# Group-norm statistics sent over ScalarE's queue, with the order of VectorE, ScalarE and TensorE changed around them

## What is computed

```python
xn = group_norm(x)                      # 32 groups of 12 channels
w  = xn^T qkv_w^T                       # (n, 384), in 12 heads of 32 channels
s  = sum_d (w / norm_n(w))^2            # per point and head
Pi = softmax over the heads (s * temp)
Pn = Pi / (sum_n Pi + 1e-8)
attn = 1 / (1 + sum_n Pn * w^2)         # per head and channel
y  = x + (-(w * Pi) * attn) out_w^T + out_b
```

## Time and profile before

| | us |
|---|---|
| median of 3 runs | 910.02 (908.9 to 911.25) |
| the profiled execution | 909.34 |
| its span, first to last instruction | 907.6 |

### The profile page before, as it was taken

One profiled execution on the slowest core, in us unless ns is written; L12 is line 12 of the kernel. 1 busy time (PEld: TensorE's weight loads), 2 busy tenths in 40 slices (PEclk: granted clock), 3 DMA queues, 4 the chain that ended last, 5 costly groups with the idle time before them and its releaser, 6 DMA issues.

```text
span 907.6 us, 14234 instructions
## 1 busy us (share of the span) xinstructions
PE 861.0 (95%) x4322; PEld 687.0 (76%) x4322; DVE 743.8 (82%) x1368; ACT 523.4 (58%) x676; POOL 225.6 (25%) x101
## 2 busy tenths in 40 slices
PE   7799999999999999999999999999999999999996
PEld 6577787777777777778777778777778777778785
DVE  7588888888888888888888888888888888888755
ACT  4566555667555667555667655567655567655621
POOL 1331133332123332123332123333123333113300
PEclk9899999999999999999999999999999999999998
DMA  7314664544665544565544565544565444464432
GB/s 286 123 46 177 216 217 154 183 143 172 214 216 165 176 144 169 211 216 175 184 142 167 197 216 188 175 148 163 192 216 203 161 160 165 179 215 148 145 120 93
DMA packets 54852, 158.47 MB, mean 175 GB/s; under 512 B 21426, under 2 KB 25778, under 8 KB 50866
## 3 DMA queue, kind: packets, MB, share of 16 engines
q1 hardware_dynamic: 54688, 158.25, 51.5%
q10 hardware_dynamic: 146, 0.00, 0.0%
HBM read 105.70 MB, written 52.53 MB: 174 GB/s over the span
## 4 chain that ended last, share of the span: by engine, by line
PE 50%; DMA 16%; issue 13%; DVE 11%; ACT 7%; SPq 2%; ACTq 1%; DVEq 0%
PE acc L482 46%; DMA PIB<-pi 12%; DMA pi<-PIT 4%; PE scores L562 3%; DVE WV L778 3%; ACT WS L386 2%; ACT XH L414 2%; ACT WV L395 1%; DVE UL L788 1%; SPq L301 1%; SPq L296 1%; ACT UH L376 1%; PE acc L465 1%; DVE WS L752 1%; DVE PIT L740 1%
## 5 line engine op out<-in xcount | busy, mean ns | idle before, releaser
L336 POOL TENSOR_TENSOR XL<-XN,XH 128x1024 fp32r<-128x1024 f32 x93 | 222.6, 2408 | 617.2 <-ACT XH L414 616.2
L386 ACT ACTIVATE WS<-acc 128x1024 f32<-128x1024 f32 x96 | 97.6, 1017 | 236.2 <-PE acc L482 177.5
L482 PE MATMUL acc<-UH,W2H 128*128 128x512 f32 x576 | 179.1, 392 | 4.5 <-ACT UH L376 4.5
L482 PE MATMUL acc<-XH,W1H 128*128 128x512 f32 x576 | 178.7, 392 | 3.7 <-ACT XH L414 3.7
L482 PE MATMUL acc<-UH,W2L 128*128 128x512 f32 x576 | 178.4, 391 | 0.0
L482 PE MATMUL acc<-XH,W1L 128*128 128x512 f32 x576 | 178.2, 391 | 0.0
L796 DVE SCALAR_TENSOR_TENSOR X<-acc,bias,X 128x1024 f32<-128x1024 f32 x96 | 120.1, 1276 | 56.9 <-PE acc L482 56.8
L376 ACT ACTIVATE UH<-WV 128x1024 fp32r<-128x1024 f32 x96 | 98.1, 1054 | 108.6 <-DVE WV L778 108.3
L482 PE MATMUL acc<-UL,W2H 128*128 128x512 f32 x576 | 150.2, 396 | 0.0
L482 PE MATMUL acc<-XL,W1H 128*128 128x512 f32 x576 | 147.0, 391 | 0.0
L752 DVE CUSTOM_DVE_ANT_0 WS<-PIB,WS 128x1024 f32<-128x1024 f32 x96 | 117.2, 1223 | 23.3 <-DMA PIB<-pi 21.7
(11 more groups left out here) (78 smaller groups left out, 443.2 us busy)
## 6 DMA issues: line engine op xcount, KB each, us to landing
PIB<-pi SPq DMA_DIRECT2D x96, 528.0 KB, 6.0
out_y<-X SPq DMA_DIRECT2D x96, 512.0 KB, 6.8
X<-in_x SPq DMA_DIRECT2D x31, 1536.0 KB, 6.2
gathered<-stats_rows SPq DMA_DIRECT2D x31, 72.0 KB, 2.8
pi<-PIT SPq DMA_DIRECT2D x96, 16.5 KB
X<-in_x SPq DMA_DIRECT2D x3, 512.0 KB, 4.5
WV<-in_L_conv_qkv_w SPq DMA_DIRECT2D x1, 576.0 KB, 6.4
WS<-in_L_conv_out_w SPq DMA_DIRECT2D x1, 576.0 KB, 7.4
```

The costliest lines, as they stand in the source:

```text
L336: pool.tensor_tensor(XL[:, t, :], XN[:, t, :], XH[:, t, :].bitcast(F32), ALU.subtract).then_inc(xl_done, 1)
L386: act.activation(square_tile(i, t), acc[:, t, :], ACT.Square, accum_out=sumsq[:, t:t + 1]).then_inc(squared, 1)
L482: last = pe.matmul(out[:, h * BANK:(h + 1) * BANK], w[:, k, m * P:(m + 1) * P], r[:, k, h * BANK:(h + 1) * BANK], start=(n == 0 and k == 0 ...
```

## The change

- `write_stats` and `gather_stats` leave SP's queue for ACT's: ACT issues both at the end of its step, after XH of tile 2. The pair of image 1 stays on SP.
- ACT: `group_seeds` moves to right behind u_hi(0); in step 0 to right behind square(2).
- DVE: `group_norm` moves ahead of the u_lo's, `head_sum_weights` ahead of u_lo(2). In the step behind the last image finish(30, 2) moves behind the three weigh's.
- Image 1: XN and XL are made by DVE, in step 0 behind the softmax and ahead of the statistics of tiles 1 and 2, instead of by ACT and POOL.
- Start: the statistics of image 1 are taken before the low parts of the second weights.
- PE, in step 0: 4 idle turns ahead of the head sums and 6 behind them.

```diff
-IDLE_TURNS = (6, 3, 4, 24)
+IDLE_TURNS = (6, 3, 4, 24, 4, 6)
@@ sync, step
                 spread_pi(i)
-                write_stats(i + 2)
                 store(i - 1, 0)
                 store(i - 1, 1)
-                gather_stats(i + 2)
@@ gpsimd, x_lo and scalar, normalise
-                if has(j) and j.follows(1):
+                if has(j) and j.follows(2):
@@ scalar, step
                 u_hi(0)
+                if i.follows(1):
+                    group_seeds(i + 1)
                 square_w(1)
                 u_hi(1)
                 u_hi(2)
                 square_w(2)
+                if has(i) and not i.follows(1):
+                    group_seeds(i + 1)
                 keep_w(1)
-                if has(i):
-                    group_seeds(i + 1)
                 keep_w(2)
...
                 x_hi(2)
+                if i.follows(0):
+                    write_stats(act, i + 2)
+                    gather_stats(act, i + 2)
@@ tensor, step
                 first_product(i, 2)
+                if not i.follows(1):
+                    idle_turns(small[:, P:2 * P], IDLE_TURNS[4])
                 second_product(i - 1, 0, {(2, 0): lambda: head_sums(i)})
+                if not i.follows(1):
+                    idle_turns(small[:, P:2 * P], IDLE_TURNS[5])
@@ vector, step
                     dot(i - 1, t)
-                if not has(i) and has(i - 1):
-                    finish(i - 2, 2)
                 for k in range(4):
                     attention(i - 1, k)
                 group_moments(i + 1)
                 weigh(i - 1, 0)
                 weigh(i - 1, 1)
                 weigh(i - 1, 2)
+                if not has(i) and has(i - 1):
+                    finish(i - 2, 2)
+                group_norm(i + 1)
                 u_lo(i - 1, 0)
                 u_lo(i - 1, 1)
+                head_sum_weights(i)
                 u_lo(i - 1, 2)
-                head_sum_weights(i)
-                group_norm(i + 1)
                 group_stats(i + 2, [0])
                 softmax_shift(i)
                 softmax_divide(i)
+                if not i.follows(1):
+                    normalise(FIRST + 1)
+                    lower_x(FIRST + 1)
                 group_stats(i + 2, range(1, T))
@@ vector, start
-            normalise_first()
-            lower_first()
+            normalise(FIRST)
+            lower_x(FIRST)
+            group_stats(FIRST + 1, range(T))
             weights_lower(range(T, 2 * T))
...
-            group_stats(FIRST + 1, range(T))
             pipeline(dve, step, 0, B + 1)
```

More of the change, by code:

```diff
@@ L234, in x_tile, with write_stats, gather_stats @@
             return X[:, j.slot, t * N:(t + 1) * N]
+        def write_stats(eng, j):
+            if has(j):
+                eng.wait_ge(gn_step, j.counts(GN_STEPS, GN_MEASURED))
+                if j.follows(2):
+                    eng.wait_ge(stats_gathered, j.counts(16, -16))
+                eng.dma_start(stats_dram, stats[:].rearrange("p k s -> p (k s)")).then_inc(stats_written, 16)
+        def gather_stats(eng, j):
+            if has(j):
+                eng.wait_ge(gn_step, j.counts(GN_STEPS, GN_AGGREGATED - GN_STEPS))
+                eng.wait_ge(stats_written, j.counts(16))
+                rows = stats_dram.rearrange("(g k) s -> g (k s)", k=PER_GROUP).unsqueeze(1)
+                eng.dma_start(gathered[:], rows.to_broadcast([GROUPS, PER_GROUP, PER_GROUP * T * HALVES * 6]))\
+                        .then_inc(stats_gathered, 16)
         def pipeline(eng, step, first, last):
@@ L264, in _ @@
                 load(Image(j, j))
[L266 to L281, removed]
             def store(j, t):
@@ L308, in step @@
                 spread_pi(i)
-                write_stats(i + 2)
                 store(i - 1, 0)
                 store(i - 1, 1)
-                gather_stats(i + 2)
-            write_stats(FIRST + 1)
-            gather_stats(FIRST + 1)
+            write_stats(sp, FIRST + 1)
+            gather_stats(sp, FIRST + 1)
             pipeline(sp, step, 0, B + 1)
@@ L682, in group_norm, with normalise, lower_x @@
                     dve.tensor_scalar(shift_j, group_mv[:, 0:1], -1.0, rstd_j, ALU.mult, ALU.mult).then_inc(gn_step, 1)
-            def normalise_first():
-                rstd_j, shift_j = norm_of(FIRST)
-                dve.wait_ge(gn_step, GN_STEPS)
+            def normalise(j):
+                rstd_j, shift_j = norm_of(j)
+                dve.wait_ge(gn_step, j.counts(GN_STEPS, GN_STEPS))
                 for t in range(T):
-                    dve.tensor_scalar(XN[:, t, :], x_tile(FIRST, t), rstd_j, shift_j, ALU.mult, ALU.add)\
+                    if j.follows(1):
+                        dve.wait_ge(xl_done, j.counts(T, t + 1 - T))
+                    dve.tensor_scalar(XN[:, t, :], x_tile(j, t), rstd_j, shift_j, ALU.mult, ALU.add)\
                         .then_inc(xn_done, 1)
-            def lower_first():
+            def lower_x(j):
                 for t in range(T):
-                    dve.wait_ge(xn_done, t + 1)
-                    dve.wait_ge(xh_done, t + 1)
+                    dve.wait_ge(xn_done, j.counts(T, t + 1))
+                    dve.wait_ge(xh_done, j.counts(T, t + 1))
+                    if j.follows(1):
+                        dve.wait_ge(m1_done, j.counts(T))
                     dve.tensor_tensor(XL[:, t, :], XN[:, t, :], XH[:, t, :].bitcast(F32), ALU.subtract)\
```

## The result

The changed kernel takes 900.18 us (median of 4 runs, 898.69 to 903.81), the kernel before beside it 910.63 (908.9 to 913.66): ratio 0.989, 95% interval 0.9845 to 0.993. It is faster, by 10.5 us, where 22 were predicted; 900.18 lies just outside the range of 882 to 900. The profiled execution took 898.69 us, with a span of 896.7 against 907.6.

A forecast was written before the change was run, and what follows sets the result against it. The prediction took a closed loop through PIB and the wait for the statistics' gather, 0.9 us longer than PE's work, as the bound: 909.34 - 23.0 (loop) + 1.9 (start) - 0.9 (end) = 887.3, hence 888 us; range 882 to 900.

The forecast's parts named there:

- the gather lands at H + 8.0 + W + 0.1 + 2.8: Loop: landing of the statistics' gather issued by ACT, in time for every W up to 6.6; wanted at H + 17.5.
- H: The start of a step's head sums on PE; from one to the next is one turn, 27.08 us on average before.
- W: Landing time of the statistics' write on ACT's queue, taken as 4 us; landings seen lie from 2.5 to 6.8.
- The turn model: Loop: each turn becomes max(26.14, old length - old wait for the gather), gaining 24.4 us, or 23.0 with PIB later.
- PIB, d = 0.1: Loop: PIB transfers land later by d beside the statistics' transfers; 0.1 us lowers the gain from 24.4 to 23.0 us.
- rival 1: Loop: PIB comes later than reckoned, d = 0.3 to 0.7; gain 19.6 to 8.8, 891 to 902 us; chance 0.17.
- rival 2: Loop: changing queue doesn't speed the statistics' write, W = 6.4; gain about 21.4, time 889 to 890 us; chance 0.10.
- the four rivals: Rivals 1 and 2; 3, slower, PIB over 1.0 us later, chance 0.03; 4, more gain, 882 to 883 us, chance 0.06.
- The start: Up to image 1's head sums: later dots, gather and weigh cost 1.9 us, from 0 to 3.5.
- The end: Last step: finish(30, 2), 1.20 us, leaves the path to PE's last product; gain 0.6 to 1.2, taken as 0.9 us.
- my 0.2 us of margin: Loop: ACT's third square in time for DVE's head-sum weights, 6.67 us against 6.90, so the seeds' move costs nothing.
- The signs: Named for right: idle before line 666 near zero, before line 562 under 8 us, H to H 26.1 to 26.3.

The follow-up runs named there:

- e4: The changed kernel with the gather on SP's queue between PIB and the stores, the write staying on ACT's: 886.56 us, ratio 0.9747.
- e5: The changed kernel with the stores of tiles 0 and 1 held until the statistics' write has landed, the gather staying on ACT's queue: 885.82 us, ratio 0.9747.
- e3: The changed kernel without the statistics' write and gather for images 2 and later, which use image 1's moments: 886.99 us, ratio 0.9743.
- e6: e4 with the start as before (image 1's part undone, no idle turns in step 0), the loop's new orders kept: 882.41 us, ratio 0.9706.
- e8: e4 without the ten idle turns of step 0: 886.53 us, one run.
- e2: The changed kernel with the statistics' write and gather back on SP's queue in their old places: 910.47 us, ratio 1.0006.
- e7: The kernel before with the write on ACT's queue and the gather on SP's ahead of the stores, no new orders: 882.78 us, ratio 0.9708.
- e1: The kernel before with only the statistics' write and gather of images 2 and up moved to ACT's queue: 901.55 us, ratio 0.9905.
- e11: e7 with 20 small memsets added to DVE's program ahead of the loop: 882.54 us, ratio 0.9717.

## Why the prediction was wrong

**The step that failed** is "the gather lands at H + 8.0 + W + 0.1 + 2.8". W was taken as 4 and measured as 4.0, and up to the issue the sum was good or better: H + 11.2 measured, 12.1 reckoned, as ACT issued the write at H + 7.3. The 2.8 came from the earlier trace rows, where every gather was issued at about H + 15.7, behind the landing of PIB and of the write, with the stores 5 to 6 us on their way. The change issues it 4 us before the last PIB transfer lands, and behind two stores of 512 KB. There it took 6.7. With 18.0 for the landing, wanted at 17.5, the wait stays, and takes 13 of the 23 us. The prediction bounded W from both sides and left this term without a bound, and nowhere did it name the stores between PIB and gather. e4 and e5 put the term back to 3.1 and 4.5 us, and both end near the forecast (886.6 and 885.8 for 888).

**The turn model held.** Turns without the wait, the late jumps aside, are 26.15 (e3, e4, e6), and PE's own turn was put at 26.14; the prediction even had 12 turns 0.17 us longer, and e6 has none. That 0.94 us of each turn could be had, and that the wait for the gather was what held it, was right: e6 gets 758.5 us from H2 to H31, for 784.5 before.

**PIB, d = 0.1.** The last PIB transfer lands at H + 15.2 at the median for 15.25 before: d was about nothing, so the 1.4 us taken for it were not due. The time lies within the numbers of rival 1 (891 to 902), but its mechanism wasn't at work; that a rival's range held the result is luck. Of rival 2 the mechanism, no quicker write, is refuted (4.0); none of the four rivals had the gather behind the stores.

**Queue or order.** The sentence of the Trainium skill ("DMA: Bandwidth & Descriptors", Issuing engines are not separate DMA queues) that another engine saves issue time only is not refuted by the write's 4.0 us for 6.4. ACT issued the write 0.3 us behind the first PIB transfer and ahead of the other two, and it landed with that first one (medians H + 11.3 and 11.2); on SP's queue it stood behind all three. No run issues it as early on SP's queue, so what the queue gave by itself isn't shown. The gather, which lands no earlier than the stores ahead of it on the other queue, agrees with the sentence. By turns packet by packet (the Trainium skill, "DMA: Bandwidth & Descriptors", Queues, rings and completion order) the gather should have moved soon after its issue. The write did: its packets run from 361.9 on, beside PIB's. The gather's did so only beside the stores, 4.3 us late; the measurement decides.

**The start** cost 0.8 us to H2 instead of 1.9. H0 came at 32.45 (32.4 predicted), and the dots began at 44.67 (44.8). But ACT issued the gather at 46.4, 1.6 us behind the write where I had counted 2.7 at least, and it had landed by 48.95: `weigh` at 49.66 for 51.1 and H1 at 57.09 for 58.9. The prediction did not have the start's second price, DVE's late jump in six turns, which shows in e3, e4, e5 and e8.

**The end** gained 1.9 us instead of 0.9. The 1.2 us of `finish` were right: from the third dot to `weigh` are 2.1 us for 3.3. Another 0.5 came from a third dot that started earlier; PE's idle before UH is 2.6 us for 4.3. And the granted clock is 0.50 for 3.4 us behind that idle, where it was for 6.8 before. The prediction left the clock open to both sides and took 0.3 off for it. How long the clock is down differs between executions of the same end (6.8 us in e4, 3.4 in e5 and e8), so part of the 1.9 us is luck.

**The margins.** After the change the third square released the head-sum weights in two steps only. In e4, where the gather no longer holds DVE, it does so 23 times, by 0.36 us mostly: my 0.2 us of margin was none. It costs nothing, since PE doesn't wait for the weights there. The reordering is neutral (e2; e6 against e7).

**The signs** named beforehand said the same at once: idle before line 666 near zero (25.6), before line 562 under 8 us (15.6), H to H at 26.1 to 26.3 (26.73). The issues alone were near what was foretold, write at H + 7.3 for 8, gather at H + 11.2 for 11 to 13.

## What to carry to other kernels

A transfer's duration in a profile belongs to what was in flight at its issue; when a change issues it earlier, ask what then stands ahead of it, on any queue, and bound that term too. Put a small urgent transfer ahead of large unhurried ones in the order of issue: here one moved line gave 2.0%, and ACT's queue without it 0.95%. Before a change of many parts, try the one move that takes the wait away.

## What the runs showed of the hardware

**Stores issued behind PIB slow it.** With the stores at H + 9.1 the last PIB transfer lands at H + 15.1, and at H + 13.7 where they go at 11.7 (e4). At the median it takes 6.8 to 6.9 us from its issue in before, after, e1, e2 and e3, where the first store goes out within 1.6 us of it, and 5.9 to 6.1 in the others, where the stores are 3 us or more behind. Stretches of 1 us of the timeline, after and then e4 (the last three columns are PEclk, DMA share and GB/s):

```profile
363.00:364.00 1.00, 1.00 (x6) 0.84 (x5) 0.41 (x1) 0.00 (x0) 0.00 (x0) 1.00 1.05 199
364.00:365.00 1.00, 1.00 (x7) 0.81 (x6) 1.00 (x2) 0.00 (x0) 0.00 (x0) 1.00 0.49 93
```

```profile
357.00:358.00 1.00, 1.00 (x6) 0.84 (x5) 0.36 (x1) 0.00 (x0) 0.00 (x0) 1.00 0.66 203
358.00:359.00 1.00, 1.00 (x6) 0.83 (x5) 1.00 (x2) 0.00 (x0) 0.00 (x0) 1.00 0.99 389
```

Two to three microseconds behind the issue of the stores the DMA engines move 93 GB/s and are busy for half of the time; the like dip in e4, where the stores are not yet out, is to 203 GB/s. What they wait for isn't shown.

**A jump back can cost its engine 0.4 to 1.4 us.** It did with 38 packets on q14 (e3, e4, e5, e8) and didn't with 9 (e7), with 38 (after, e2) or with 40 (e11), so the code ahead of the loop has a part in it, and the count of packets alone doesn't tell. Their time does: late are the kernels whose instruction packet starts at H + 9.8 or later, behind a hundred and more of PIB's.
